# First expert layer of a gated cross-attention kernel: twelve full blocks from five of eight groups of tokens, the rest from a second block list

## What is computed

```python
x = x + tanh(g_xattn[0]) * L0_xattn(layernorm(x), ctx, ctx, ...)     # 77 keys of 192 columns
# _L0_ffn_ref(layernorm(x), gate_w, w1, w2, w3): 8 experts, 512 hidden columns, 2 of 8 per token
probs = softmax(xf @ gate_w.T)
weights, idx = top_k(probs, 2); weights /= weights.sum(-1)
out_all[e] = (silu(xf @ w1[e].T) * (xf @ w3[e].T)) @ w2[e].T
x = x + tanh(g_ffn[0]) * sum_k(weights[k] * out_all[idx[k]])
# layer 1: cross-attention with 16 heads, then 8 experts that each pick 256 tokens per sequence
```

## Time and profile before

| | us |
|---|---|
| median of 3 runs | 1499.35 |
| lowest and highest | 1499.15, 1502.27 |
| profiled execution | 1504.12 |
| its span, first to last instruction | 1502.4 |

### The profile page before, as it was taken

One profiled execution on the slowest core, in us unless ns is written; L12 is line 12 of the kernel. 1 busy time (PEld: TensorE's weight loads), 2 busy tenths in 40 slices (PEclk: granted clock), 3 DMA queues, 4 the chain that ended last, 5 costly groups with the idle time before them and its releaser, 6 DMA issues.

```text
span 1502.4 us, 30586 instructions
## 1 busy us (share of the span) xinstructions
PE 1287.4 (86%) x9764; PEld 972.3 (65%) x9765; DVE 963.4 (64%) x2090; ACT 644.2 (43%) x2032; POOL 629.1 (42%) x643
## 2 busy tenths in 40 slices
PE   6875169999999988899999920289999999999997
PEld 3764158899999957788888820135666555666555
DVE  2897436555555476788888879566655666655651
ACT  3774123333232355888888830033333333333321
POOL 2277736666666530454544440312233332233213
PEclk8666579999999999999999965599999999999998
DMA  4666125543434350001010120232233332242212
GB/s 140 208 165 187 29 50 127 85 67 60 66 60 67 55 130 2 15 29 35 28 35 28 36 105 0 65 117 71 71 109 82 81 80 70 70 113 37 35 14 29
DMA packets 75076, 107.14 MB, mean 71 GB/s; under 512 B 20278, under 2 KB 66876, under 8 KB 71932
## 3 DMA queue, kind: packets, MB, share of 16 engines
q0 software_dynamic: 29312, 37.31, 15.3%
q1 hardware_dynamic: 44700, 68.62, 14.4%
q10 hardware_dynamic: 992, 0.27, 0.1%
HBM read 69.65 MB, written 36.52 MB: 71 GB/s over the span
## 4 chain that ended last, share of the span: by engine, by line
PE 73%; issue 11%; DVE 6%; ACT 3%; DMA 3%; POOL 2%; SPq 0%; POOLq 0%; another core or an unknown queue 0%; DVEq 0%; ACTq 0%
PE psG L122 6%; PE psG L123 6%; PE psG L124 6%; PE psU L122 6%; PE psU L123 6%; PE psU L124 6%; PE psYb L122 4%; PE psYb L123 4%; PE psYb L124 4%; PE psS L122 2%; PE psS L123 2%; PE psS L124 2%; PE psP L1412 2%; PE psY L122 2%; PE psY L124 2%
## 5 line engine op out<-in xcount | busy, mean ns | idle before, releaser
L1705 POOL DMA_INDIRECT out_x<-yo,gidx x64 | 100.9, 1577 | 328.1 <-ACT yo L1789 318.4
L1819 DVE SCALAR_TENSOR_TENSOR hid<-psU,sil 128x512 f32<-128x512 f32 x128 | 88.5, 691 | 188.9 <-ACT sil L1778 188.1
L922 POOL DMA_INDIRECT x_rows<-yo,tabs x78 | 124.3, 1593 | 110.4 <-ACT yo L985 90.4
L1778 ACT ACTIVATE sil<-psG 128x512 f32<-128x512 f32 x128 | 76.4, 597 | 216.5 <-PE psU L124 200.1
L1359 ACT ACTIVATE pr<-psS,mx 128x77 f32<-128x77 f32 x512 | 158.3, 343 | 5.9 <-DVE mx L1491 4.1
L122 PE MATMUL psYb<-W1h,hh 128*128 128x256 f16 x512 | 139.6, 273 | 0.0
L123 PE MATMUL psYb<-W1l,hh 128*128 128x256 f16 x512 | 139.6, 273 | 0.0
L124 PE MATMUL psYb<-W1h,hl 128*128 128x256 f16 x512 | 139.6, 273 | 0.0
L1012 DVE SCALAR_TENSOR_TENSOR hid<-psU,sil 128x512 f32<-128x512 f32 x78 | 53.8, 690 | 126.5 <-ACT sil L976 124.8
L1359 ACT ACTIVATION_READ_ACCUMULATOR pr<-psS,mx 128x1 f32 x512 | 115.1, 225 | 0.0
L1696 POOL DMA_INDIRECT gx<-n_rows,gidx x64 | 66.4, 1038 | 101.0 <-DVE gidx L1669 58.6
(11 more groups left out here) (324 smaller groups left out, 3991.7 us busy)
## 6 DMA issues: line engine op xcount, KB each, us to landing
w1s<-in_w SPq DMA_DIRECT2D x16, 1536.0 KB, 6.3
stage<-in_w SPq DMA_DIRECT2D x8, 1536.0 KB
X<-in_x SPq DMA_DIRECT2D x8, 512.0 KB, 8.7
n_rows<-xc SPq DMA_DIRECT2D x8, 512.0 KB
x_rows<-X SPq DMA_DIRECT2D x8, 512.0 KB
X<-x_rows SPq DMA_DIRECT2D x8, 512.0 KB, 8.3
out_x<-X SPq DMA_DIRECT2D x32, 128.0 KB, 1.7
n_rows<-xn SPq DMA_DIRECT2D x32, 128.0 KB, 1.8
```

The lines of the kernel that those rows point to most:

```text
L922: pool.indirect_dma_start(x1_rows[:, :], bass.IndirectOffsetOnAxis(tabs[:, j, n, 0:1], 0), yo[:, par, n, :], None, compute_op=ALU.add).the ...
L1705: pool.indirect_dma_start(out_rows[:, :], bass.IndirectOffsetOnAxis(gidx[:, half, col:col + 1], 0), yo1[:, j % 2, n, :], None, compute_op= ...
L1778: act.activation(sil1[:, f % 2, :], psG1[f % 2][:], ACT.Silu, scale=1.0 / (SX * SW)).then_inc(d_sil, 1)
L1819: dve.scalar_tensor_tensor(hid1[:, f % 2, :], psU1[f % 2][:], SH / (SX * SW), sil1[:, f % 2, :], ALU.mult, ALU.mult).then_inc(d_hid, 1)
```

## The change

- Groups 0 to 4 (GE = 5) are scattered in the attention pipeline as before, but a group's first three tiles in step j - 5 and its last tile one step later, between the two rstd instructions' steps of GpSimd. `slots` has a buffer for each group, and place waits for no scatter any more.
- After group 4 VectorE makes an early list of NBE = (2 * 5 * 512 - 8 * 255) // 256 = 12 blocks, which counts whole blocks of each expert only (14 semaphore steps: one after add_base, the rest one step later).
- SyncE's waits ahead of table 0 are those for groups 0 to 4. The waits for the rest and the two small loads stand ahead of table 12; FIRST_PIECE is 10.
- GpSimd scatters groups 5 to 7 in the expert layer: two tiles ahead of gather 0, then one or two tiles behind each of gathers 1 to 9. Gather 0 waits for seven experts' Wl, add 0 for all stored x1 rows.
- VectorE makes the late list (19 semaphore steps) behind block 0's and block 1's work: the blocks that the early list has not taken, from each expert's first open block on.
- Some small tiles and `tabs` move to allocations that live through both stages.

The diff, without the moved allocations; block_counts, experts_of and place_blocks are the old chain's instructions cut into functions:

```diff
+GE = 5
+NBE = (2 * GE * GT * P - E * (BR - 1)) // BR
...
-                      ("add_base", 5), ("low_in", 1), ("values_low", 2), ("own_ranks", 5), ("weight_second", 5),
-                      ("own_rows", 5), ("place", 5), ("shift_out", 3), ("weights_low1", 4), ("top_logits", 4),
+                      ("add_base", 5), ("early_counts", 5), ("low_in", 1), ("values_low", 2), ("own_ranks", 5), ("weight_second", 5),
+                      ("own_rows", 5), ("place", 5), ("early_list", 6), ("shift_out", 3), ("weights_low1", 4), ("top_logits", 4),
...
-        POOL0_ORDER = [("rstd_out", 3), ("rstd_in", 0), ("scatter", 5)]
+        POOL0_ORDER = [("rstd_out", 3), ("scatter_last", 6), ("rstd_in", 0), ("scatter", 5)]
...
             for n in range(2):
-                sp.wait_ge(s_n0[n], 16 * (NG // 2))
-            sp.wait_ge(s_keep, 16 * NG)
+                sp.wait_ge(s_n0[n], 16 * ((GE + 1 - n) // 2))
+            sp.wait_ge(s_blk, EARLY_STEPS)
+            sp.wait_ge(s_sct[0], 16 * 2 * GT * GE)
...
+        def scatter_tile(pool, g, k):
+            for c in range(2):
+                pool.indirect_dma_start(tab[:, :], bass.IndirectOffsetOnAxis(slots[:, g, c, k:k + 1], 0),
+                                        tokw[:, GT * g + k, c, :], None, bounds_check=E * REG - 1,
+                                        oob_is_err=True).then_inc(s_sct[g // GE], 16)
+
+        def scatter_ready(pool, g):
+            pool.wait_ge(s_slot, g + 1)
+            pool.wait_ge(s_wt, 4 * g + 4)
...
+            steps = dict(rstd_out=rstd_of(1), rstd_in=rstd_of(0), scatter=scatter(range(3)), scatter_last=scatter(range(3, GT)))
...
                 dve.wait_ge(s_row, 4 * g + 4)
-                wait(dve, s_sct[par], 16 * 2 * GT * (g // 2))
-                dve.tensor_copy(slots[:, par, :, :], slotf[:]).then_inc(s_slot, 1)
+                dve.tensor_copy(slots[:, g, :, :], slotf[:]).then_inc(s_slot, 1)
...
+            def early_counts(g, par):
+                if g != GE - 1:
+                    return
+                dve.wait_ge(s_row, 4 * g + 2)
+                early(dve.scalar_tensor_tensor(cnt[:], base[:], float(1 - BR), reg8[:], ALU.add, ALU.subtract))
+
+            def early_list(g, par):
+                if g != GE - 1:
+                    return
+                block_counts(dve, early)
+                done = done_of(NBE)
+                cols = slice(0, NBE)
+                experts_of(dve, early, done, nblk, cols)
+                early(dve.tensor_tensor(mj[:, cols], iotaj[:, cols], mj[:, cols], ALU.subtract))
+                early(dve.tensor_scalar(mj[:, cols], mj[:, cols], float(BR), None, ALU.mult))
+                place_blocks(dve, early, cols)
...
-        FIRST_PIECE = 4
+        FIRST_PIECE = 10
...
             def load_table(j, par):
+                if isinstance(j, int) and j == NBE:
+                    sp.wait_ge(s_blk, EARLY_STEPS + LATE_STEPS)
+                    sp.wait_ge(s_sct[1], 16 * 2 * GT * (NG - GE))
+                    for n in range(2):
+                        sp.wait_ge(s_n0[n], 16 * (NG // 2))
+                    sp.dma_start(gts1[:], a["gate1"]).then_inc(b_w1, 16)
+                    sp.dma_start(bo[:], a["bo1"]).then_inc(b_w1, 16)
...
-            sp.wait_ge(s_blk, 15)
-            for n in range(2):
-                sp.wait_ge(s_sct[n], 16 * T)
-            sp.dma_start(gts1[:], a["gate1"]).then_inc(b_w1, 16)
-            sp.dma_start(bo[:], a["bo1"]).then_inc(b_w1, 16)
...
+        LATE_SCATTERS = {1: (2,), 2: (3, 4), 3: (5,), 4: (6,), 5: (7,), 6: (8,), 7: (9,), 8: (10,), 9: (11,)}
...
                 pool.wait_ge(b_tab[par], 16 * (j // 2) + 16)
+                if j == 0:
+                    pool.wait_ge(s_wl, 2 * (E - 1))
...
                 pool.wait_ge(b_yo, j + 1)
+                if j == 0:
+                    pool.wait_ge(s_keep, 16 * NG)
...
-            pipeline(pool, NB0, BDEPTH, [(0, gather), (3, add)], straight=True)
+            def late_scatter(j, ph):
+                for n in LATE_SCATTERS.get(j, ()):
+                    g, k = GE + n // GT, n % GT
+                    scatter_ready(pool, g)
+                    scatter_tile(pool, g, k)
+            scatter_ready(pool, GE)
+            for k in range(2):
+                scatter_tile(pool, GE, k)
+            pipeline(pool, NB0, BDEPTH, [(0, gather), (0, late_scatter), (3, add)], straight=True)
...
+                if j == 0:
+                    dve.wait_ge(s_row, 4 * NG - 2)
+                    late(dve.tensor_scalar(most[:, 1:E + 1], cum[:], float(NBE), None, ALU.min))
+                    late(dve.tensor_tensor(taken[:, 0:E], most[:, 1:E + 1], most[:, 0:E], ALU.subtract))
+                    late(dve.tensor_tensor(cnt[:], base[:], reg8[:], ALU.subtract))
+                    block_counts(dve, late)
+                if j == 1:
+                    experts_of(dve, late, done, start, cols)
+                    late(dve.scalar_tensor_tensor(mj[:, cols], iotaj[:, 0:NB0 - NBE], taken[:, 0:1], mj[:, cols], ALU.add, ALU.subtract))
+                    late(dve.tensor_scalar(lt[:, cols], ej[:, cols], float(E), float(BR), ALU.is_lt, ALU.mult))
+                    late(dve.tensor_tensor(mj[:, cols], mj[:, cols], lt[:, cols], ALU.mult))
+                    place_blocks(dve, late, cols)
+                    late.end()
+            pipeline(dve, NB0, PEEL, [(2, hidden(0)), (1, rows_low), (2, hidden(1)), (1, low_piece), (2, late_list)])
```

More of the change, by code:

```diff
@@ L170, in program @@
         blkw = sb("blkw", [P, NB0], I32, l0)
+        thr = sb("thr", [P, E, B * S // BR], F32, l0)
+        tri8 = sb("tri8", [P, E, E], F32, l0)
+        iotaj = sb("iotaj", [P, NB0], F32, l0)
+        base = sb("base", [P, E], F32, l0)
+        reg8 = sb("reg8", [P, E], F32, l0)
+        cnt = sb("cnt", [P, E], F32, l0)
+        more = sb("more", [P, E, B * S // BR], F32, l0)
+        nblk = sb("nblk", [P, E], F32, l0)
+        tri8n = sb("tri8n", [P, E, E], F32, l0)
+        cum = sb("cum", [P, E], F32, l0)
+        ej = sb("ej", [P, NB0], F32, l0)
+        mj = sb("mj", [P, NB0], F32, l0)
+        lt = sb("lt", [P, NB0], F32, l0)
+        tokw = sb("tokw", [P, T, 2, 2], I32, l0)
+        slots = sb("slots", [P, NG, 2, GT], I32, l0)
+        most = sb("most", [P, E + 1], F32, l0)
+        taken = sb("taken", [P, E + 1], F32, l0)
+        rest = sb("rest", [P, E], F32, l0)
+        start = sb("start", [P, E], F32, l0)
         a0 = ExitStack()
@@ L367, in attn0_gpsimd @@
             pool.memset(mhalf[:], -0.5)
+            pool.memset(most[:, 0:1], 0.0)
+            pool.memset(taken[:, E:E + 1], 0.0)
             ch(pool.memset(onesb[:], 1.0))
@@ L396, in rstd_of, with scatter, run @@
                 return run
[L398 to L408, removed]
+            def scatter(tiles):
+                def run(g, par):
+                    if g >= GE:
+                        return
+                    scatter_ready(pool, g)
+                    if g == 0:
+                        pool.wait_ge(s_tab, 16 * 3)
+                    for k in tiles:
+                        scatter_tile(pool, g, k)
+                return run
+            steps = dict(rstd_out=rstd_of(1), rstd_in=rstd_of(0), scatter=scatter(range(3)), scatter_last=scatter(range(3, GT)))
             in_order(pool, steps, POOL0_ORDER, NG, straight=True)
@@ L776, in values_low @@
                        .then_inc(s_setdve, 1)
+            early = Chain(dve, s_blk, 0, EARLY_STEPS)
+            def early_counts(g, par):
[5 more added lines that the diff above has]
+                if g != GE - 1:
+                    return
+                block_counts(dve, early)
[5 more added lines that the diff above has]
+                place_blocks(dve, early, cols)
+                early.end()
             steps = dict(values_low=values_low, stats_in=after_first(stats(0)), stats_out=stats(1), shift_in=after_first(shift_of(0)), shift_out=shift_of(1),
@@ L1030, in low_piece, with late_list @@
                 ins.then_inc(b_w1l, 1)
-            pipeline(dve, NB0, PEEL, [(2, hidden(0)), (1, rows_low), (2, hidden(1)), (1, low_piece)])
+            late = Chain(dve, s_blk, EARLY_STEPS, 1)
+            late.steps = LATE_STEPS
+            cols = slice(NBE, NB0)
+            done = done_of(NB0 - NBE)
+            def late_list(j, par):
+                if not isinstance(j, int):
+                    return
+                if j == 0:
[12 more added lines that the diff above has]
+            pipeline(dve, NB0, PEEL, [(2, hidden(0)), (1, rows_low), (2, hidden(1)), (1, low_piece), (2, late_list)])
         l0.close()
```

69 lines of the change are left out of this document (31 added, 38 removed).

## The result

| | us |
|---|---|
| changed kernel, median of 5 runs | 1485.52 (1480.98 to 1490.25) |
| kernel before, median of 5 runs | 1500.39 (1499.15 to 1502.27) |
| ratio | 0.9895, 95% interval [0.9878, 0.9912] |
| profiled execution, its span | 1480.98, 1479.2 |

The change gains 1.1%, 14.9 us, where 31.7 were forecast. The profiled pair differs by more, 23.1 us: behind block 38 the kernel before took 986.1 us in its profile and the changed one 980.4, and in all twenty traces of this case that part takes 979.9 to 986.4, whatever the kernel. One execution of half_scatters, further down, took 2012.83 us at a granted clock of 0.638, where all others have 0.905 to 0.924; it is left out.

The account below looks back on a forecast made before the run. TensorE was taken to bound the middle of the expert layer, with a hole ahead of block 0. Start 34.7 less 2.5 for late scatters and 0.5 for pieces gives 31.7 us: 1499.35 - 31.7 = 1467.7 us, range 1462 to 1478.

Parts of the forecast that it names:

- Start: Block 0 of the expert layer: transposes at 163.1 instead of 197.79, 34.7 us earlier.
- Attention's end: TensorE finishes attention at about 162.4 instead of 164.05, just before block 0's rows land.
- the early list: VectorE's block list on 12 columns, in attention's idle time: 3.5 us, costing 1.0 us hidden behind the landing.
- table 12: SyncE's stop before this table for all scatters and the late list: 7.8 us, hidden by three blocks of 8.3.
- the late list: 20 VectorE instructions behind blocks 0 and 1: cost 0, or 1.9 us if TensorE's cover is gone.
- the pieces: Layer 1's pieces move from blocks 5 to 9 to 11 to 15: 0.5 us added (0 to 1.5).
- The late scatters: GpSimd's 24 remaining scatters overfill six expert-layer periods by 0.55 us each; TensorE stall taken as 2.5 us, 0 to 4.0.
- My upper row: Late scatters at the mean duration beside attention, 1.175 + 0.30: 0.90 us over in six periods, 4.0 us lost.
- Rival 1: GpSimd becomes the bound, each late scatter waiting for a VectorE instruction: 10.2 us lost, 1475.4 us; chance 0.12.
- Rivals 2 to 5: Later block 0, about 1474 (0.10); more gain, 1464 (0.10); TensorE clock low, 1567 (0.03); no effect, 1499 (0.02).

Follow-up runs that it names:

- half_scatters: Changed kernel with every second late scatter (those of the second choice) left out; 1468.17 us, three runs, chip 13.
- no_late: Changed kernel without the scatters of groups 5 to 7 and the wait for them; 1468.47 us, chip 2.
- pool_busy: Changed kernel with each of the 24 late scatters replaced by a small GpSimd power operation (128x3); 1466.79 us, chip 3.
- packed: Changed kernel with late scatters moved forward: none before gather 0, three tiles in each of steps 1 to 3, one in each of 4 to 6; 1476.02 us, chip 3.
- spaced: Changed kernel with no scatter ahead of gather 0; one, two, three late tiles in steps 0 to 2, one in each of 3 to 8; 1476.23 us, chip 13.
- singles: Changed kernel, no scatter ahead of gather 0, late tiles in steps 0 to 4, the last three one scatter at a time in steps 5 to 10; 1473.2 us, chip 13.
- no_front: Changed kernel with only the first two late tiles moved, from ahead of gather 0 into step 1; 1471.91 us, chip 13.
- again: The changed kernel unchanged, run once more on chip 2; 1483.18 us.
- control: The changed kernel unchanged, run on chip 13; 1470.9 us.
- tables_spread: Changed kernel with table loads 4 to 11 each held back to the transposes of the block four before; 1482.35 us, chip 2.
- no_front_b: Changed kernel with its first two late tiles moved from ahead of gather 0 into step 1, run on chip 6; 1489.09 us.
- small_reads: Changed kernel with each of the 24 late scatters replaced by an indirect read of the same 8-byte entries; 1474.03 us, chip 3.
- no_adds: Changed kernel with the 156 accumulating adds of the experts' results replaced by small fills; 1464.76 us, one run, chip 3.
- adds_full: Changed kernel with each add of the experts' results replaced by a GpSimd power operation of 128x10; 1470.75 us, one run, chip 13.

## Why the prediction was wrong

- **Start, 34.7.** Measured 32.8 by the transposes. SyncE went out at 156.13 (156.4 forecast), but table 0 took 4.8 us to gather 0 where I had 2.1. It took 2.3 to 2.4 in all forms without small transfers ahead of gather 0 (no_late, pool_busy, packed, spaced, singles, no_front), and 2.6 to 5.0 in those with them. I had priced those four scatters by their issue, "covered by the table's way"; by these runs they stand in that way. The whole effect is 0.3 to 2.7 us.
- **Attention's end, the early list, table 12, the late list, the pieces.** The last ranks end at 163.7, where I had 162.4 and the kernel before 164.05: of the 1.6 us forecast here 0.3 came, which costs nothing because the rows land later. The list takes 147.5 to 150.9 (3.4 us of 3.5), gather 12 waits for nothing, and the pieces cost what they cost before. The late list costs nothing that shows: blocks 0 to 38 take 317.5 us in no_late, which has it, and 317.3 before.
- **The late scatters, 2.5 (0 to 4.0).** This is the step that failed. It priced only the overrun of GpSimd's issue and had no term for what a scatter's transfer holds up. In the first result and on chips 2 and 6, TensorE stands still in the middle of products and its signals reach the other engines up to 7.0 us behind the recorded ends. Blocks 0 to 38 take 13 to 16 us more than before, and the whole term is 14.7 us by again against no_late.
- **The same step on chip 13.** There its mechanism holds: GpSimd's issue is overfull and TensorE waits for gathered rows. Blocks 5 to 11 take 4.0 us more than without late scatters, and the kernel takes 1470.9 us, in the range. The size was still too small for the 2.5 that I took. The 2.05 us that I took for idle contain the 0.30 that stands ahead of every issue, so 1.75 were free. Two scatters take 2.63 in the control's rows, and the overrun is 0.9 and not 0.55. My upper row has the same 0.90 by luck: it came from scatters of 1.175 us, and these took 1.0.
- **Rivals.** Rival 1 named the right engine and the right place, and its 1475.4 lies nearer, but scatters took 1.0 us each among the blocks, not 1.7. Trainium skill, SBUF — State Buffer, "SBUF: two separate sides", speaks of the lock behind it. The traces agree elsewhere: in the changed kernel a scatter of 2.64 us starts at 131.86, 0.08 us behind a VectorE instruction of 1.75. Among blocks 0 to 11 no scatter shows it. Rivals 2 to 5 didn't occur; granted clock and the other stages are as forecast.

The trace of before could have told some of this. Its list of waits from 0 to 150 us has one line that no instruction explains:

```profile
DVE rank L726 <- remote: 0.9, 2, 0.4
```

It is small, and it is where 14 of 33 signals of TensorE are late, from the start of the scatters on. I moved these scatters from a stage that can bear late signals into one that TensorE bounds, and did not look for them.

What stays open: why TensorE's signals are late on some chips and not on others. Shown are the conditions: late signals come with the scatters, in attention as among the blocks (none ahead of the first scatter, none among blocks 0 to 11 of no_late, which has gathers and adds but no scatters there), the table loads and the scatters ahead of gather 0 don't matter (tables_spread, no_front_b), and all kernels of a batch are alike. Whether it is the chip itself or something else that lasts as long as a batch is not told apart; chip 13 was free of it in two batches, the other chips ran one each. small_reads, no_adds and packed all ran on chip 3, adds_full on 13; on a chip of the paired kind neither reads in place of writes, nor single scatters, nor leaving out the adds were tried, so which of them the paired form needs is not known.

## What to carry to other kernels

Price a moved DMA twice: once for its issue on its engine (here 1.3 us for a scatter; two of them, two gathers and two adds in a period of 8.3 make 9.2), and once for what its transfer holds up, above all for the engine that bounds the stage it moves into. From a wait before an instruction take off the 0.30 us that stand ahead of it anyway. Where the engine that issues has less idle time in a period than two issues take, put one in: on chip 13 single scatters cost nothing and pairs up to 1.0 us each; on the chips of the paired form pairs cost 1.8 and singles were not tried. And run the unchanged kernel in every batch: eight forms, run without it on other chips, looked like the proof of a cure until the control stood beside them.

## What the hardware showed that I had not expected

- The same program takes 1470.9 us on one chip and 1483 to 1487 on two others, each in all its executions, while the kernel before takes 1499 us on all of them. In the slower form TensorE's signals are late while scatters of 128 x 8 bytes run, in the kernel before as well, and in the faster form never. Granted clock is no part of it (0.917 and 0.918 in the two profiles of the control).
- Scatters of 8 bytes from each of 128 partitions land in 3.7 to 4.4 us at the median, 4.4 to 6.2 at most, in the traces of chips 3 and 13 that record it; reads of the same entries in 2.3. In the paired form no trace records it.
- Small power operations on GpSimd take 0.85 us for 128x3, 1.04 for 128x4 (beside attention), 1.49 for 128x7 and 1.97 for 128x10. Stand-ins for issue time have to be measured before they are used; two of mine were too short.
